# The imaginary half of an autocorrelation product, moved from VectorE to GpSimd by way of a ScalarE copy

## The chip, the cores and the metric

The kernel runs on one core of a Trainium2 chip. The metric is the device time of one launch in microseconds (us). The kernel of before took 1334.72 us, the median of 3 runs (1332.58 to 1335.19).

## What is computed

The program is a decoder of two blocks over 8 batches of 128 positions by 512 channels. The change lies in one step of its first block, the autocorrelation attention of `x` over a context:

```python
qf = jnp.fft.fft(q, axis=2)
kf = jnp.fft.fft(k, axis=2)
corr = jnp.fft.ifft(qf * jnp.conj(kf), axis=2).real
w, idx = jax.lax.top_k(corr.transpose(0, 1, 3, 2), topk)   # topk = int(2 ln 128) = 9
w = jax.nn.softmax(w, axis=-1)
for i in range(topk):
    g = jnp.minimum(idx[:, :, None, :, i] + pos, L - 1)
    out = out + w[:, :, None, :, i] * jnp.take_along_axis(v, g, axis=2)
```

The kernel does this sum with Fourier matrices. The weights (nine entries a channel, zero elsewhere) and the values are both taken to the frequency domain, multiplied there as complex numbers, and taken back by four matmuls.

## The kernel before, in words

The program is written engine by engine: each engine has its own list of instructions, which it works through strictly in order, and semaphores carry the data dependencies. What comes earlier in the program (a state-space model) ends at about 505 us of the span. Then comes the correlation stage, up to about 640 us, with one iteration for each batch b from 0 to 7. Its pieces, with their lines, are these.

On TensorE (PE): `values(b)` (L706, L707) takes the context to its spectrum in banks 1 and 2; `spectra(b)` (L688) does so for x in bank 0; `correlate(b)` (L696, L697) makes the correlation in bank 3; `turn_weights(b)` (L713) transposes the chosen weights; `weights(b)` (L723, L724) takes them to their real spectrum in bank 5 and their imaginary spectrum in bank 6, and raises `wf_done`; `aggregate(b)` (L731) makes four 128x512 matmuls over `m4` into bank 7 and raises `xat_done`. Pieces of the output projection of the stage before (`out_proj`, L647), the small matmuls of the feed-forward layer (`lora_update`, L758), its transposes (`turn`, L739) and its matmuls (`ffn`, L747) stand between them. In iteration b the order is `turn_weights(b)`, `weights(b)`, `correlate(b+1)`, some `out_proj`, `values(b+2)`, `aggregate(b)`, `spectra(b+2)`. In the last iteration `ffn(0)` stands ahead of `turn_weights(7)`, and `ffn(1)` and a `turn` stand ahead of `aggregate(7)`.

On VectorE (DVE): `spectra(b)` (L1830) multiplies the two spectra and waits for PE's `spectra(b)`; `products(b)` (L1873, L1874) multiplies the value spectrum `vri[b % 2]` (128 x 2 x 512, in SBUF) by the real and by the imaginary spectrum of the weights, each read from PSUM, into the four planes of `m4`; `topk(b)` (L1838 to L1863) finds nine maxima and normalises; `out_ln(b)` and `x_ln(b)` add a projection to the token tile and take its statistics (`ln_a`, L1652 to L1656), `ln_b` (L1660) normalises once GpSimd has raised `ln_rs`; `tables(0..2)` are chains of small operations on 4 columns (`tables(2)` is L1630 to L1639). In iteration b the order is `spectra(b+1)`, some `ln_b` and `out_ln`, `x_ln(b-1)`, `products(b)`, `topk(b+1)`. Iteration 4 has `out_ln(7)` behind its `topk(5)`; iteration 6 has `effective()` (L1887) between `products(6)` and `topk(7)`. After the loop stand `ln_b(1,6)`, then `ln_a(2,0)` and `ln_a(2,1)`, the sums behind `ffn(0)` and `ffn(1)`, and only then `x_ln(7)`.

On ScalarE (ACT), all through the helper `av` (L1035): the exponentials of `topk` (`exponents`), six copies in `values(b)`, two of them into `vri[b % 2]`, and the copy of the transposed weights (`turned_weights`).

On GpSimd (POOL) the stage has small work: `rstd` (L1391), one `pow` on one column for each normalisation, in a fixed order; four dequantising rounds k = 0 to 3 (L1483 to L1485), each followed by `rstd(1, k)`; then `rstd(0, 7)` and `table_start` (L1493 to L1496); then for b = 4 to 7 `rstd(1, b)` and two (for b = 7 one) of the doubling rounds of a table (L1504 to L1509). For b = 7 two `bias` additions (L1520) and `rstd(2, 0)` and `rstd(2, 1)` come ahead of `rstd(1, 7)`. `rstd(s, b)` waits for the statistics of DVE's `ln_a(s, b)`. The SP queue issues the loads; none of its waits is on the products.

The loop on GpSimd, as it stands in the kernel of before:

```python
rstd(pool, 0, B - 1)          # waits for DVE's out_ln(7)
table_start()
for b in range(KD, B):        # b = 4..7
    if b == B - 1:
        ...
        for i in range(2): bias(i, i, "fbias")
        for i in range(2): rstd(pool, 2, i)
    rstd(pool, 1, b)
    for k in rounds[2 * (b - KD):2 * (b - KD) + 2]: table_round(k)
```

Of the kernel before, what the change touches and what calls it, by code (L numbers as in the profile page):

```python
# [11 lines left out]
ALU = mybir.AluOpType  # L12
ACT = mybir.ActivationFunctionType
AX = mybir.AxisListType

P = 128
B = 8
L = 128
D = 512
# [126 lines left out]
def decoder_kernel(nc, xT, xtok, ctxT, ctxtok, par, rows, four, win, wx, wdt, wout, qw, sc, ze,  # L146
# [3 lines left out]
    with ExitStack() as ctx:  # L150
# [29 lines left out]
        def part(at, size, parts=P):  # L180
            return arena[0:parts, int(at * KB):int(at * KB) + size]
# [19 lines left out]
        bank = [psum[:, i * 512:(i + 1) * 512] for i in range(8)]  # L201
# [56 lines left out]
        wn = part(36, 2 * D).rearrange("p (s n) -> p s n", s=2)  # L258
        wT = part(40, D)
        vri = [part(at, 2 * D).rearrange("p (i n) -> p i n", i=2) for at in (42, 58)]  # L260
        m4 = part(46, 4 * D).rearrange("p (i n) -> p i n", i=4)
        mx8 = part(54, 4 * 8)
        nx8 = part(54.25, 4 * 8)
# [24 lines left out]
        with nc.sbuf_tensor("dwout_sb", [P, D], F32) as dwout_rows:  # L288
# [47 lines left out]
            "dt_done", "dtu_done", "dA_done", "bu_done", "scan_done", "h_turned", "h_act", "h_dve", "skip_used", "ysum", "y_done",  # L336
            "wout_done",
            "x_sum", "ln_ve", "ln_rs", "x_done",
            "kk_sb", "qf_done", "m12_done", "corr", "rep_done", "ee_done", "wn_done",
            "vf_done", "vri_sb", "wT_done", "wT_sb", "wf_done", "m4_done", "xat_done",  # L340
            "lora_done", "weff_done", "xTt", "xT_sb", "xbias", "ffn_done",
            "tab_a", "tab_b", "tab_c", "tab_d", "tab_e", "tab_done",
# [6 lines left out]
        S = type("S", (), ls)  # L349
# [8 lines left out]
        def lnc(stage, b):  # L358

            if stage < 3:  # L360
                return norms.index((stage, b)) + 1
            if stage == 4 and b >= HB:
                return stage * B + HB + b + 1
            if stage == 5 and b < HB:
                return stage * B - HB + b + 1
            return stage * B + b + 1
# [175 lines left out]
        def _(pe):  # L542
# [122 lines left out]
            for k in range(NR):  # L665
# [6 lines left out]
                if k >= OUT_AT and (k - OUT_AT) % 10 < MD:  # L672
                    b, at = (k - OUT_AT) // 10, (k - OUT_AT) % 10
# [41 lines left out]

            def weights(b):
                if b >= 1:
                    pe.wait_ge(S.m4_done, b)
                else:
                    pe.wait_ge(S.x_sum, lnc(0, HB - 1))  # L720
                    pe.wait_ge(S.y_done, 2 * MD)
                pe.wait_ge(S.wT_sb, b + 1)
                mm(bank[5][:, :], fm["w_re"], wT, start=True, stop=True)  # L723
                mm(bank[6][:, :], fm["w_im"], wT, start=True, stop=True).then_inc(S.wf_done, 1)  # L724

            def aggregate(b):
                pe.wait_ge(S.m4_done, b + 1)
                if b >= 1:
                    pe.wait_ge(S.x_sum, lnc(1, b - 1))
                for i, k in enumerate(("o_rr", "o_ri", "o_ir", "o_ii")):  # L730
                    last = mm(bank[7][:, :], fm[k], m4[:, i, :], start=(i == 0), stop=(i == 3))  # L731
                last.then_inc(S.xat_done, 1)
# [36 lines left out]
            for b in range(B):  # L769
# [10 lines left out]
                if b == 4:  # L780
                    out_proj(7, (4,), 4)
                weights(b)
                if b + 1 < B:
                    correlate(b + 1)
# [189 lines left out]
            for s in range(SLOTS):  # L974
                v, b = s // HB, s % HB
# [57 lines left out]
        def _(act):  # L1033
            def av(o, i, f, **k):
                return nc.scalar.activation(o, i, f, **k)  # L1035
# [166 lines left out]
            def exponents(b):  # L1202
                act.wait_ge(S.rep_done, b + 1)
                for t in range(KD):
                    last = av(ee[:, t * P:(t + 1) * P], bank[3][:, t * P:(t + 1) * P], ACT.Exp, bias=negmax[:, t:t + 1])
                last.then_inc(S.ee_done, 1)

            def values(b):
                act.wait_ge(S.vf_done, b + 1)
                if b >= 1:  # L1210
                    act.wait_ge(S.m12_done, b)
                h = P // 2
                av(kk[0:h, 0, :], bank[1][0:h, :], ACT.Identity)
                av(kk[h:P, 1, :], bank[1][0:h, :], ACT.Identity)
                av(kk[h:P, 0, :], bank[2][0:h, :], ACT.Identity)
                av(kk[0:h, 1, :], bank[2][0:h, :], ACT.Identity).then_inc(S.kk_sb, 1)
                if b >= 2:
                    act.wait_ge(S.m4_done, b - 1)
                av(vri[b % 2][:, 0, :], bank[1][:, :], ACT.Identity)
                av(vri[b % 2][:, 1, :], bank[2][:, :], ACT.Identity).then_inc(S.vri_sb, 1)  # L1220

            def turned_weights(b):
                act.wait_ge(S.wT_done, b + 1)
                av(wT, bank[3][:, :], ACT.Identity).then_inc(S.wT_sb, 1)
# [5 lines left out]
            def turned(b, n, bk):  # L1230
                act.wait_ge(S.xTt, n + 1)
                av(x2T[:, :, b * L:(b + 1) * L], bank[bk][:, :].rearrange("p (k t) -> p k t", k=KD),
                   ACT.Identity).then_inc(S.xT_sb, 1)

            for b in range(B):
                if b == B - 1:
                    turned(0, 0, 0)
                    turned(1, 1, 1)
                turned_weights(b)
                if b + 1 < B:  # L1240
                    exponents(b + 1)
                if b + 2 < B:
                    values(b + 2)
                if b == 0:
                    act.wait_ge(S.tab_a, 1)
                    av(tsm[:, 8, :], tsm[:, 7, :], ACT.Tanh).then_inc(S.tab_b, 1)
# [107 lines left out]
            for s in range(SLOTS):  # L1354
                v, b = s // HB, s % HB
# [32 lines left out]
        def rstd(pool, stage, b):  # L1388

            pool.wait_ge(S.ln_ve, lnc(stage, b))  # L1390
            nc.gpsimd.tensor_tensor(lnrs[:, b:b + 1], lnve[:, b:b + 1], halfneg[:, 0:1], ALU.pow).then_inc(S.ln_rs, 1)  # L1391

        @block.gpsimd
        def _(pool):
            gp = nc.gpsimd
            chain = [0]

            def link(ins):
                chain[0] += 1
                ins.then_inc(S.pool_chain, 1)  # L1400
                pool.wait_ge(S.pool_chain, chain[0])
# [29 lines left out]
            for p in range(MD):  # L1431
                rest_in(p)
                if p >= 4:
                    k = p - 4
# [19 lines left out]
            for i in range(2 * MD * GS):  # L1454
                j, q, e = i // (2 * GS), i // 2 % GS, i % 2
                k = j * NS + q * NG
# [18 lines left out]
            gp.tensor_tensor(tsm[:, 5, :], tsm[:, 4, :], halfneg[:, 0:DEPTH], ALU.pow).then_inc(S.tab_d, 1)  # L1475
            rstd(pool, 0, HB)

            pool.wait_ge(S.sz_in, 64)
            for k in range(KD):
                if k in (0, 2):  # L1480
                    rstd(pool, 0, 5 + k // 2)
                pool.wait_ge(S.qw_in, 16 * (k + 1))
                link(gp.tensor_copy(weff[:, k, :], qw_sb[:, 0, :]))  # L1483
                link(gp.tensor_tensor(weff[:, k, :], weff[:, k, :], sz[:, 1, k, :], ALU.subtract))
                gp.tensor_tensor(weff[:, k, :], weff[:, k, :], sz[:, 0, k, :], ALU.mult).then_inc(S.deq_done, 1)  # L1485
                rstd(pool, 1, k)
# [11 lines left out]
            def table_round(k):  # L1498
                sh = [P, DEPTH, k]
                cl, sl = ctab[:, :, 1:k + 1], stab[:, :, 1:k + 1]  # L1500
                ck, sk = ctab[:, :, k:k + 1].to_broadcast(sh), stab[:, :, k:k + 1].to_broadcast(sh)
                cn, sn = ctab[:, :, k + 1:2 * k + 1], stab[:, :, k + 1:2 * k + 1]
                t0, t1 = ttmp[:, 0, :, 0:k], ttmp[:, 1, :, 0:k]
                gp.tensor_tensor(cn, cl, ck, ALU.mult)  # L1504
                gp.tensor_tensor(t0, sl, sk, ALU.mult)
                gp.tensor_tensor(sn, sl, ck, ALU.mult)
                link(gp.tensor_tensor(t1, cl, sk, ALU.mult))
                gp.tensor_tensor(cn, cn, t0, ALU.subtract)
                link(gp.tensor_tensor(sn, sn, t1, ALU.add))  # L1509
# [7 lines left out]
            def bias(b, n, name):  # L1517

                pool.wait_ge(S.xTt, n + 1)
                gp.tensor_tensor(x_tok[:, b, :], x_tok[:, b, :], rw(name), ALU.add).then_inc(S.xbias, 1)  # L1520
# [4 lines left out]
            for b in range(KD, B):  # L1525
                if b == B - 1:
                    pool.wait_ge(S.row_in, 16)
                    for i in range(2):
                        bias(i, i, "fbias")
                    for i in range(2):  # L1530
                        rstd(pool, 2, i)
                rstd(pool, 1, b)
                for k in rounds[2 * (b - KD):2 * (b - KD) + 2]:
                    table_round(k)
# [35 lines left out]
            for s in range(SLOTS):  # L1570
# [9 lines left out]
                rv, b = (s - 4) // HB, (s - 4) % HB  # L1580
# [7 lines left out]
        def _(dve):  # L1588
            v = nc.vector
# [277 lines left out]
            def products(b):  # L1867
                dve.wait_ge(S.wf_done, b + 1)
                dve.wait_ge(S.vri_sb, b + 1)
                if b >= 1:  # L1870
                    dve.wait_ge(S.xat_done, b)

                v.tensor_tensor(m4[:, 0:2, :], vri[b % 2], bank[5][:, :].unsqueeze(1).to_broadcast([P, 2, D]), ALU.mult)  # L1873
                v.tensor_tensor(m4[:, 2:4, :], vri[b % 2], bank[6][:, :].unsqueeze(1).to_broadcast([P, 2, D]),  # L1874
                                ALU.mult).then_inc(S.m4_done, 1)

            def out_ln(b):
# [208 lines left out]
            for s in range(SLOTS):  # L2086
# [10 lines left out]
                if 4 <= s < NU * HB + 4:  # L2097
                    r = s - 4
                    rv, rb = r // HB, r % HB
                    if rv % NKV == NKV - 1:  # L2100
                        b = (rv // NKV) * HB + rb
# [79 lines left out]
```

## Time and profile before

| | before |
|---|---|
| median of 3 runs | 1334.72 us |
| profiled execution, its own time | 1333.96 us |
| its span, first to last instruction | 1332.2 us |
| PE busy | 1236.0 us (93%) |
| DVE busy | 968.5 us (73%) |
| ACT busy | 748.2 us (56%) |
| POOL busy | 674.8 us (51%) |
| mean granted TensorE clock | 0.986 of full |

Times in views are microseconds from the start of the span. Busy shares are averages over stages; what the stage of the change is limited by has to be read from its own rows. The chain of waits is the sequence of work that ended last, followed back from the end; an instruction that stands in it would move the end if it moved, until something else comes later. Matmuls are pipelined, so in the timeline a matmul's record begins up to 0.2 us ahead of the same piece in the chain.

### The profile page before, as it was taken

What the parts mean: (1) busy time and instruction counts of PE and PEld (TensorE: products, weight loads), DVE (VectorE), ACT (ScalarE), POOL (GpSimd) and SP (SyncE); (2) the same over time, 40 slices, a digit from 0 to 9 for tenths busy, and PEclk for the clock granted to TensorE, in tenths of its full rate; (3) what the DMA queues carried; (4) which work ended last, traced back from release to release, by engine and by line L of the source; (5) the groups of instructions that cost most, each with busy time, mean ns of one, the idle gap of its engine ahead of it and who ended that gap; (6) DMA issues with size and microseconds to landing.
All of it is one profiled execution on the core that took longest, in us unless ns stands there. A gap on an engine that the chain in (4) does not pass through costs nothing.

```text
span 1332.2 us, 18653 instructions
## 1 busy us (share of the span) xinstructions
PE 1236.0 (93%) x6464; PEld 925.4 (69%) x6464; DVE 968.5 (73%) x1770; ACT 748.2 (56%) x1478; POOL 674.8 (51%) x535
## 2 busy tenths in 40 slices
PE   6997899999998988998998999999998999999995
PEld 5876677767777764444565547888887888888874
DVE  4785798999999997898657766655554675666676
ACT  5479898989998983332133235544544445444441
POOL 4128988888988870222842126443433543333331
PEclk9999899999999999999999999999998999999999
DMA  6003200122220015002300103222221221111110
GB/s 182 12 26 139 75 25 25 35 93 88 88 72 1 1 56 136 16 9 85 144 9 16 40 24 103 80 73 71 68 75 48 80 79 65 63 64 64 48 48 32
DMA packets 37213, 81.92 MB, mean 61 GB/s; under 512 B 3808, under 2 KB 8160, under 8 KB 35200
## 3 DMA queue, kind: packets, MB, share of 16 engines
q1 hardware_dynamic: 37120, 80.72, 18.5%
q8 instruction: 53, 0.87, 0.3%
q14 instruction: 40, 0.33, 0.1%
HBM read 74.35 MB, written 6.36 MB: 61 GB/s over the span
## 4 chain that ended last, share of the span: by engine, by line
PE 68%; DVE 19%; ACT 6%; issue 5%; POOL 1%; DMA 1%; SPq 1%; DVEq 0%; POOLq 0%; ACTq 0%
PE psum L547 10%; PE psum L549 10%; PE psum L548 10%; PE psum L622 7%; PE psum L636 6%; PE psum L982 4%; DVE arena L1747 4%; PE psum L660 3%; PE psum L647 3%; ACT arena L1035 3%; PE psum L747 2%; PE psum L1001 2%; PE psum L731 1%; DVE lnst L1654 1%; PE psum L871 1%
## 5 line engine op out<-in xcount | busy, mean ns | idle before, releaser
L1471 POOL TENSOR_TENSOR arena<-arena 128x1024 f32<-128x1024 f32 x128 | 300.4, 2370 | 42.7 <-DVE arena L1747 42.5
L1407 POOL TENSOR_TENSOR w_split<-arena,w_split 128x512 fp32r<-128x512 f32 x128 | 168.1, 1333 | 280.3 <-ACT w_split L1035 280.3
L1747 DVE TENSOR_TENSOR_SCAN arena<-psum,arena 128x512 f32<-128x512 f32 x256 | 292.3, 1204 | 15.2 <-ACT psum L1035 15.2
L622 PEld LDWEIGHTS psum<-prm,arena 128*128 128x128 f32 x1024 | 118.7, 142 | 110.3 <-issue 61.8
L1035 ACT ACTIVATE psum<-arena,amat 128x508 f32<-128x508 f32 x256 | 173.3, 709 | 30.4 <-DVE arena L1747 29.4
L622 PE MATMUL psum<-prm,arena 128*128 128x128 f32 x1024 | 148.9, 280 | 38.4 <-DVE arena L1747 34.7
L1035 ACT ACTIVATE arena<-psum,ssmC 128x256 f32<-128x256 f32 x448 | 177.5, 484 | 10.8 <-PE psum L622 10.7
L1035 ACT ACTIVATE arena<-arena 128x512 f32<-128x512 f32 (+2 forms) x86 | 62.8, 734 | 210.1 <-DVE arena L2043 209.1
L1035 ACT ACTIVATE arena<-psum,prm 128x512 f32<-128x512 f32 (+1 forms) x130 | 91.1, 708 | 148.6 <-PE psum L549 70.0
L636 PE MATMUL psum<-prm,arena 128*128 128x128 f32 x1024 | 134.1, 273 | 0.1
L636 PEld LDWEIGHTS psum<-prm,arena 128*128 128x128 f32 x1024 | 117.0, 141 | 0.4 <-ACT arena L1035 0.3
L547 PE MATMUL psum<-x_split,w_split 128*128 128x512 f32 x256 | 106.3, 415 | 2.9 <-DVE x_split L2029 2.8
L1035 ACT ACTIVATE arena<-psum 128x512 f32<-128x512 f32 (+4 forms) x108 | 57.8, 563 | 82.7 <-PE psum L739 33.3
L1391 POOL TENSOR_TENSOR lnrs<-lnve,halfneg 128x1 f32<-128x1 f32 x48 | 28.4, 591 | 143.3 <-DVE lnve L1656 143.3
L549 PE MATMUL psum<-x_split,w_split 128*128 128x512 f32 x256 | 100.9, 394 | 0.0
L548 PE MATMUL psum<-x_split,w_split 128*128 128x512 f32 x256 | 100.8, 394 | 0.0
L547 PE MATMUL psum<-w_split,o_split 128*128 128x512 f32 x256 | 100.7, 394 | 0.0
L549 PE MATMUL psum<-w_split,o_split 128*128 128x512 f32 x256 | 100.1, 391 | 0.0
L548 PE MATMUL psum<-w_split,o_split 128*128 128x512 f32 x256 | 99.6, 389 | 0.0
L2040 DVE TENSOR_REDUCE amax<-psum 128x4 f32<-128x512 f32 x64 | 44.1, 688 | 52.4 <-PE psum L982 52.4
L2059 DVE TENSOR_TENSOR ssmT<-psum,p_split 128x512 fp32r<-128x512 f32 x64 | 44.2, 691 | 51.5 <-ACT p_split L1035 51.4
L2049 DVE TENSOR_REDUCE asum<-arena 128x4 f32<-128x512 f32 x64 | 43.9, 686 | 44.0 <-ACT arena L1035 44.0
(230 smaller groups left out, 2544.0 us busy)
## 6 DMA issues: line engine op xcount, KB each, us to landing
arena<-wq SPq DMA_DIRECT2D x64, 256.0 KB, 2.6
arena<-wo SPq DMA_DIRECT2D x64, 256.0 KB, 2.8
arena<-bc_scratch SPq DMA_DIRECT2D x8, 1024.0 KB, 5.2
arena<-win SPq DMA_DIRECT2D x16, 256.0 KB, 2.7
v_keep<-row SPq DMA_DIRECT2D x16, 256.0 KB, 2.1
arena<-v_keep SPq DMA_DIRECT2D x1, 4096.0 KB, 12.8
arena<-xT SPq DMA_DIRECT2D x8, 256.0 KB, 5.5
x_tok<-wv SPq DMA_DIRECT2D x1, 2048.0 KB, 7.7
```

The lines of the kernel that those rows point to most:

```text
L547: mm(o, l[0], r[0], start=start, stop=False)
L548: mm(o, l[0], r[1], start=False, stop=False)
L549: return mm(o, l[1], r[0], start=False, stop=stop)
L622: last = nc.tensor.transpose(hT[:, c, b % 2, e, :], hst[:, (2 * k + e) % 4, b * L:(b + 1) * L], ident)
L636: last = mm(bank[6 + e][:, b * L:(b + 1) * L], hTs[:, k % 2, b, e, :], ident, start=(n == 0 and b == 0), stop=(n == NS - 1 and b == HB - 1 ...
L982: last = mm(bank[1][:, j * P:(j + 1) * P], qT[:, v % 2, j, b * L:(b + 1) * L], KT[:, v % NKV, gb * L:(gb + 1) * L], start=True, stop=True)
L1035: return nc.scalar.activation(o, i, f, **k)
L1407: gp.tensor_tensor(out_, whole, hi.bitcast(F32), ALU.subtract).then_inc(done, 1)
L1471: gp.tensor_tensor(bu[:, i % 4, :, :], dtu[:, (2 * j + e) % 4, :].unsqueeze(1).to_broadcast([P, NG, HT]), Brep[:, q * NG:(q + 1) * NG, :], ...
L1747: v.tensor_tensor_scan(hst[:, i % 4, :], decay_bank(i), bu[:, (k // NG * 2 + e) % 4, k % NG, :], 0.0, ALU.mult, ALU.add).then_inc(S.scan_d ...
L2040: link(v.tensor_reduce(amax[:, :], ps, AX.X, ALU.max))
L2059: v.tensor_tensor(p_lo[:, r % 2, :], bank[2][:, :], p_hi[:, r % 2, :].bitcast(F32), ALU.subtract).then_inc(S.p_rest, 1)
```

## The change

`wim` is a new tile of 128x512 in SBUF. ScalarE copies bank 6, the weights' imaginary spectrum, into it, behind `turned_weights(b)` in its list. GpSimd multiplies `vri[b % 2]` by `wim` into planes 2 and 3 of `m4` (`imaginary(b)`). VectorE keeps planes 0 and 1. Both engines raise `m4_done`, which so counts two for each batch, and every wait on it is doubled.

```diff
+        wim = part(62, D)
...
             def weights(b):
                 if b >= 1:
-                    pe.wait_ge(S.m4_done, b)
+                    pe.wait_ge(S.m4_done, 2 * b)
...
             def aggregate(b):
-                pe.wait_ge(S.m4_done, b + 1)
+                pe.wait_ge(S.m4_done, 2 * (b + 1))
...
                 if b >= 2:
-                    act.wait_ge(S.m4_done, b - 1)
+                    act.wait_ge(S.m4_done, 2 * (b - 1))
                 av(vri[b % 2][:, 0, :], bank[1][:, :], ACT.Identity)
...
                 turned_weights(b)
+                act.wait_ge(S.wf_done, b + 1)
+                if b >= 1:
+                    act.wait_ge(S.m4_done, 2 * b)
+                av(wim, bank[6][:, :], ACT.Identity).then_inc(S.wim_sb, 1)
                 if b + 1 < B:
                     exponents(b + 1)
...
+            def imaginary(b):
+
+                pool.wait_ge(S.wim_sb, b + 1)
+                pool.wait_ge(S.vri_sb, b + 1)
+                if b >= 1:
+                    pool.wait_ge(S.xat_done, b)
+                gp.tensor_tensor(m4[:, 2:4, :], vri[b % 2], wim.unsqueeze(1).to_broadcast([P, 2, D]),
+                                 ALU.mult).then_inc(S.m4_done, 1)
+
             pool.wait_ge(S.sz_in, 64)
             for k in range(KD):
+                imaginary(k)
                 if k in (0, 2):
                     rstd(pool, 0, 5 + k // 2)
                 pool.wait_ge(S.qw_in, 16 * (k + 1))
...
                     for i in range(2):
                         rstd(pool, 2, i)
+                imaginary(b)
                 rstd(pool, 1, b)
                 for k in rounds[2 * (b - KD):2 * (b - KD) + 2]:
                     table_round(k)
...
-                v.tensor_tensor(m4[:, 0:2, :], vri[b % 2], bank[5][:, :].unsqueeze(1).to_broadcast([P, 2, D]), ALU.mult)
-                v.tensor_tensor(m4[:, 2:4, :], vri[b % 2], bank[6][:, :].unsqueeze(1).to_broadcast([P, 2, D]),
+                v.tensor_tensor(m4[:, 0:2, :], vri[b % 2], bank[5][:, :].unsqueeze(1).to_broadcast([P, 2, D]),
                                 ALU.mult).then_inc(S.m4_done, 1)
```

## Rows read from the trace of the kernel before

**Rows 1.** The page's part 4: shares of the chain that ended last, by engine
```profile
PE 68%; DVE 19%; ACT 6%; issue 5%; POOL 1%; DMA 1%; SPq 1%; DVEq 0%; POOLq 0%; ACTq 0%
```

**Rows 2.** Busy time in stretches: us, then PE, PEld, DVE, ACT, POOL, clock, DMA
```profile
560.00:590.00 30.00, 28.39 (x96) 14.61 (x95) 28.43 (x84) 9.66 (x22) 8.32 (x9) 1.00 0.04 10
```

**Rows 3.** Lines L1874 and L1471 by themselves: ns min/median/max, first and last start
```profile
L1874 DVE TENSOR_TENSOR arena<-arena,psum x8: 1214/1214/1216, 528.1 to 634.8; 128x1024 f32<-128x1024 f32 x8
L1471 POOL TENSOR_TENSOR arena<-arena x128: 2340/2365/2585, 122.3 to 490.9; 128x1024 f32<-128x1024 f32 x128
```

**Rows 4.** Chain of waits, 550 to 640 us: start us, us, what
```profile
550.25 3.43 PE psum L731 x8
...
553.69 0.87 PE psum L688 x2
...
569.20 0.64 PE psum L713 x4
...
587.70 1.22 DVE arena L1873
...
598.47 1.22 DVE arena L1830
...
601.84 1.22 DVE arena L1873
...
611.53 0.64 PE psum L713 x4
...
612.93 1.97 PE psum L723 x2
614.90 1.68 PE psum L724 x2
...
637.49 3.44 PE psum L731 x8
```

**Rows 5.** Timeline of GpSimd, 525 to 642 us: start us, us, engine, line, operation, tiles
```profile
525.05 0.55 POOL L1391 TENSOR_TENSOR lnrs<-lnve,halfneg 128x1 f32<-128x1 f32 x1
...
547.56 0.55 POOL L1391 TENSOR_TENSOR lnrs<-lnve,halfneg 128x1 f32<-128x1 f32 x1
...
558.58 0.55 POOL L1391 TENSOR_TENSOR lnrs<-lnve,halfneg 128x1 f32<-128x1 f32 x1 [4.65 <-DVE lnve L1656]
...
598.60 0.55 POOL L1391 TENSOR_TENSOR lnrs<-lnve,halfneg 128x1 f32<-128x1 f32 x1 [10.22 <-DVE lnve L1656]
...
599.29 0.19 POOL L1496 COPY arena<-tsm 128x4 f32<-128x4 f32 x1
602.03 0.55 POOL L1391 TENSOR_TENSOR lnrs<-lnve,halfneg 128x1 f32<-128x1 f32 x1 [2.54 <-DVE lnve L1656]
...
604.95 0.21 POOL L1509 TENSOR_TENSOR arena<-arena 128x8 f32<-128x8 f32 x1
...
631.79 0.55 POOL L1391 TENSOR_TENSOR lnrs<-lnve,halfneg 128x1 f32<-128x1 f32 x1 [13.73 <-DVE lnve L1656]
...
641.86 0.55 POOL L1391 TENSOR_TENSOR lnrs<-lnve,halfneg 128x1 f32<-128x1 f32 x1 [1.20 <-DVE lnve L1656]
```

**Rows 6.** Timeline of VectorE in tables(2) and products(2), 558 to 561 us
```profile
558.42 0.15 DVE L1630 TENSOR_TENSOR tsm<-tsm 128x4 f32<-128x4 f32 x1
...
559.97 1.22 DVE L1873 TENSOR_TENSOR arena<-arena,psum 128x1024 f32<-128x1024 f32 x1
```

**Rows 7.** Timeline at 1275 us: a VectorE operation with two SBUF inputs beside GpSimd
```profile
1275.14 1.28 POOL L1407 TENSOR_TENSOR w_split<-arena,w_split 128x512 fp32r<-128x512 f32 x1 [4.44 <-ACT w_split L1035]
...
1275.51 1.47 DVE L2053 TENSOR_TENSOR arena<-arena,ainv 128x512 f32<-128x512 f32 x1
```

**Rows 8.** Timeline of TensorE, weights(5) and turn_weights(6)
```profile
598.54 1.10 PE L723 MATMUL psum<-arena 128*128 128x512 f32 x2 [0.78 <-ACT arena L1035]
...
611.53 0.63 PE L713 MATMUL psum<-prm,arena 128*128 128x128 f32 x4 [2.73 <-DVE arena L1863]
```

**Rows 9.** Busy time at 613 us: us, PE, PEld, DVE, ACT, POOL, clock, DMA
```profile
613.00:614.00 1.00, 1.00 (x2) 0.48 (x3) 0.96 (x2) 0.00 (x0) 0.00 (x0) 0.51 0.00 0
```

More of the change, by code:

```diff
@@ L338, in decoder_kernel @@
             "x_sum", "ln_ve", "ln_rs", "x_done",
-            "kk_sb", "qf_done", "m12_done", "corr", "rep_done", "ee_done", "wn_done",
+            "kk_sb", "wim_sb", "qf_done", "m12_done", "corr", "rep_done", "ee_done", "wn_done",
             "vf_done", "vri_sb", "wT_done", "wT_sb", "wf_done", "m4_done", "xat_done",
```

## The prediction

> **What bounds the kernel now.** I read the page's chain first: PE holds 68% of it and DVE 19%, GpSimd 1% [rows 1]. That average hides the stage of the change, so I went to the busy time of a stretch inside it: from 560 to 590 us PE is busy 28.39 us of 30 and DVE 28.43, GpSimd only 8.32 [rows 2]. Two engines are the bound there together. The chain of waits says the same: it changes between them, and DVE's product and PE's matmuls take turns in it, from 587.70 on for one [rows 4]. So a shorter DVE list can gain something, and the idle share of GpSimd looks like free room. But GpSimd works its list in order, so the question is where each `imaginary(b)` stands in it and what stands ahead of it. That is read from GpSimd's timeline [rows 5], against the start of the `aggregate` that waits for it [rows 4].
>
> **What is removed.** L1874, 8 times. One takes 1.21 us [rows 3]; the next operation starts 1.13 us behind its start, since records overlap, so 1.13 is what goes. If DVE were the bound throughout, that would be 8 x 1.13 = 9.0 us.
>
> **What is added.** GpSimd gets 8 products of 128x1024 f32 with one operand broadcast. L1471 is the same form: 2.37 us, at most 2.59 [rows 3]. ScalarE gets 8 copies of one bank. They are hidden: the equal copy of `turned_weights`, with the steps to and from it, fits into the 0.78 us that PE idles between L713 and L723 [rows 8], and GpSimd takes up each product later than that behind wf_done in every iteration below (b = 0, where it does not, has the time). A new wait of ScalarE on wf_done has behind it only `exponents(b+1)`, which DVE's maxima release several us later. No DMA is added and SP waits for none of this.
>
> **The walk, batch by batch.** I shift the starts of before by what has been gained or lost so far. GpSimd to PE is taken as 0.15 us, the step that the chain shows from other engines to PE.
>
> b = 0: GpSimd is free at 525.6 [rows 5], the product ends at 528.0, and PE wants it behind out_proj, 7 us later. Nothing. DVE's gain goes into its wait for PE's next `spectra`.
>
> b = 1: GpSimd comes to it after rstd(1,0) at 547.56. It ends at 547.56 + 0.5 + 2.37 = 550.43, PE starts at 550.6, where before it started at 550.25 [rows 4, 5]. PE, which starts `spectra(3)` behind it (553.69), is 0.35 us late, and DVE with it.
>
> b = 2: rstd(1,1) starts at 558.58 + 0.35, so the product runs from 559.4 to 561.8. DVE is then in `tables(2)`, shifted by 0.35 from 558.42 and up to products(2) at 559.97 [rows 6], small operations most of which read two SBUF tiles. What such an operation does beside a running GpSimd one stands at 1275 us [rows 7]: L2053 took 1.47 us and ended 0.56 us behind it, where the shortest of its kind takes 0.69; it did its work only when GpSimd had finished. Against that stands that the short `pow` at 525.05 held nobody visibly. I take the first [rows 7], since 2.37 us of streaming is nearer to that than a pow on one column. The rest of the table chain then starts at 561.8, `products(2)` at 562.6 in place of 559.97, 2.65 late, and less the 1.13 saved `topk(3)` is 1.5 late. Its end releases PE's `turn_weights(3)` (569.20) [rows 4]. **+1.5 us.** Bounds: without the block PE bounds instead, 0.6 early; with a second block it is 2 us more.
>
> The Trainium skill, "SBUF — State Buffer", section "SBUF: two separate sides", states that VectorE and GpSimd share one pair of ports as an exclusive lock, for a VectorE operation with two SBUF inputs against a GpSimd one that reads SBUF, whatever its size. By this rule the term is +1.5, and by the pow row read alone -0.6; the trace at 1275 us agrees with the rule.
>
> b = 3: the product runs behind rstd(1,2), and ends 0.2 to 0.4 us ahead of PE. Nothing; the shift stays.
>
> b = 4 is the large one. `imaginary(4)` stands behind `rstd(0, 7)`, which waits for `out_ln(7)`, which DVE does only after `topk(5)`. products(4) starts at 587.70 and that rstd at 598.60 [rows 4, 5]: 10.9 us, now 10.9 - 1.13 = 9.77. Then rstd and table_start 0.88 (to 599.48), the product 2.37, the step 0.15, `aggregate(4)` 3.43, `spectra(6)` 0.87, the step to DVE 0.05: 17.52 us from products(4) to DVE's spectra(6). Before it was 598.47 - 587.70 = 10.77. **+6.75 us.** PE idles some 8 us, and while it does `vri`'s next copies wait too, without effect.
>
> b = 5: products(5) to `turn_weights(6)` was 611.53 - 601.84 = 9.69 us, bound by DVE's topk. Now rstd(1,4) starts 0.19 behind products(5), and two table rounds, to 605.16, stand ahead of the product: 0.19 + 3.13 + 2.37 + 0.15, then aggregate 3.43 and spectra(7) 0.87 make 10.14. **+0.45 us.**
>
> b = 6: before, PE's clock fell after 2.73 us of idle [rows 8] and 0.78 more, with a short transpose between: the granted clock at 613 us is 0.51, which is the 1.2 GHz level [rows 9]; L723's and L724's pairs took 1.97 + 1.68 = 3.65 us [rows 4], where at the level of 2.4 GHz they take 1.10 [rows 8] and 0.87, as L688's [rows 4], together 1.97. Now PE has 4.3 us of work just ahead of it, so I take the loss as gone: **-1.7 us** (bounds -1.7 and 0). The product ends just with lora_update, no more.
>
> b = 7: `imaginary(7)` stands behind rstd(1,6), two rounds, two bias additions and rstd(2,0), rstd(2,1). From 631.79 to 641.86 that is 10.07 us [rows 5], then 0.5 + 2.37 + 0.15 = 13.1 us to `aggregate(7)`. Before, that started at 637.49, 5.7 us behind 631.79. **+7.4 us.** From there PE is continuous to the end of the stage, so it stays.
>
> Sum: 1.5 + 6.75 + 0.45 - 1.7 + 7.4 = 14.4 us. **Clock:** the two new holes, some 8 us ahead of aggregate(4) and 7 us ahead of aggregate(7), are longer than what made the clock fall at 613 us; I charge each 1.7 us, what that fall cost (bounds 0 and twice that), +3.4. Total +17.8. The profiled execution took 1333.96 us, 0.8 under the median of its runs; the forecast is 1333.96 + 17.8 = 1351.8 us.
>
> **Rivals.**
>
> A. The order on GpSimd holds, but there is no block and little clock loss: 14.4 - 2.1 + 0 to 1.7, 1346 to 1348 us. For: small operations ran beside the pow. Against: [rows 7].
>
> B. More is lost: low clock for twice as long at each hole (+3.4), a further fall at the hole of b = 5 (some 2.4 us, +1.7), GpSimd's products blocked by DVE's two-input steps of topk. 1353.5 to 1357 us.
>
> C. GpSimd runs beside DVE and only DVE's list counts. DVE's 9.0 us come off where DVE bounds, which the chain shows for b = 2 to 5 [rows 4], about half: 1329 us; with all of it 1325. It needs each product to be done 2.5 us or so behind wf_done. It turns on the position of rstd(0,7): it would hold if `out_ln(7)` were ahead of topk(5). The list says it is not.
>
> D. The change costs and gains nothing: PE alone bounds, and the products are done in time. 1333 to 1336. The 7 us at b = 4 and b = 7 speak against it equally.
>
> **Chances.** The main case 0.55, A 0.2, B 0.17, C 0.05, D 0.03. About 0.2% (2.7 us) is what a measurement of this kernel can tell. The range takes in A and B: 1346 to 1357. Faster 0.05, same 0.03, slower 0.92.
>
> **What would show it.** In the changed kernel's timeline, GpSimd's new product should start right behind L1496's table copies for b = 4 and behind rstd(2,1) for b = 7; PE should name GpSimd's new line as the releaser of L731, with waits near 8 and 7 us; the granted clock should be near 0.5 at both; one operation of tables(2) should last some 2 us. ACT's exponents should move with DVE alone. Wrong it would be if PE's wait for those two aggregates were under 2 us each, if the chain did not pass through GpSimd, or if the stages behind 664 us had changed their length.

## The result

The changed kernel took 1359.99 us (median; 1357.98 to 1360.71 in 4 runs), the kernel before 1334.4 us beside it: a ratio of 1.0182, with a 95% interval of 1.0163 to 1.0201. The forecast was 1351.8 us, in a range of 1346 to 1357. The direction and the mechanism came as forecast, the size did not: the time lies 3 us above the range. The profiled execution took 1357.98 us, 24.0 more than the profiled execution of before (17.8 were forecast).

The page of the changed kernel shows its span, granted clock and chain. The lines of code have moved: `aggregate` is now L732, VectorE's `spectra` L1846, the ScalarE helper L1036, GpSimd's `rstd` L1396; the new product is L1489.

```profile
span 1356.2 us, 18675 instructions
...
PEclk9998999999999999988999999999998999999999
...
PE 65%; DVE 19%; ACT 5%; issue 5%; POOL 3%; DMA 1%; SPq 1%; DVEq 0%; POOLq 0%; ACTq 0%
```

GpSimd has gone from 1% of the chain [rows 1] to 3%, and the clock string has two 8s side by side at 576 to 644 us, where the kernel before has 9s. Who waits for the new product is told by its own line and by TensorE's waits from 545 to 662 us (us in total, times, longest):

```profile
L1489 POOL TENSOR_TENSOR arena<-arena x8: 2340/2344/2351, 525.8 to 655.7; 128x1024 f32<-128x1024 f32 x8
```

```profile
PE psum L732 <- POOL arena L1489: 15.7, 5, 7.7
PE psum L714 <- DVE arena L1879: 2.7, 2, 2.1
```

The product itself takes 2.34 us, as its form in [rows 3] promised. TensorE waits 15.7 us for it, in five waits. It is not that the product is slow; it starts late. GpSimd's timeline shows what stands ahead of it for batch 4 and for batch 7:

```profile
591.41 0.55 POOL L1396 TENSOR_TENSOR lnrs<-lnve,halfneg 128x1 f32<-128x1 f32 x1 [7.44 <-DVE lnve L1672]
601.52 0.55 POOL L1396 TENSOR_TENSOR lnrs<-lnve,halfneg 128x1 f32<-128x1 f32 x1 [9.55 <-DVE lnve L1672]
...
602.49 2.34 POOL L1489 TENSOR_TENSOR arena<-arena 128x1024 f32<-128x1024 f32 x1
...
644.05 0.55 POOL L1396 TENSOR_TENSOR lnrs<-lnve,halfneg 128x1 f32<-128x1 f32 x1 [9.35 <-DVE lnve L1672]
...
655.19 0.55 POOL L1396 TENSOR_TENSOR lnrs<-lnve,halfneg 128x1 f32<-128x1 f32 x1 [1.20 <-DVE lnve L1672]
655.70 2.34 POOL L1489 TENSOR_TENSOR arena<-arena 128x1024 f32<-128x1024 f32 x1
```

By 601.52 GpSimd had idled 9.55 us in its queue, with the data of product 4 ready since ScalarE's copy of 591.10 to 591.70 us: what it waited for is the statistics of `out_ln(7)`. These rows answer to 598.60 and to 631.79 and 641.86 in [rows 5].

**A measure for one stage.** The rest of the kernel (the span less the stage) took 1177.1 to 1183.1 us in the profiled executions of the runs below, though none edits it, so I measure the stage alone: from the start of the first `spectra` on VectorE to the start of the last feed-forward matmul. Both are read from the lines by themselves ("first and last start"), here of the changed kernel:

```profile
L1846 DVE TENSOR_TENSOR arena<-arena,psum x8: 1214/1222/1223, 509.7 to 625.6; 128x1024 f32<-128x1024 f32 x8
```

```profile
L748 PE MATMUL psum<-arena x64: 592/592/697, 642.4 to 685.0; 128*128 128x512 f32 x64
```

685.0 - 509.7 = 175.3 us. In the kernel before it is 662.7 - 509.5 = 153.2. So 22.1 of the 24.0 us are in this stage. Each stage length comes from one profiled execution: a fall of the clock that some executions have and others have not would stand in it with 1.7 us or more. One of the ten runs of e3_four took 3217.93 us for a cause that is not known; it does not enter the ratio. The shifts against before, counted from the first `spectra`, at the points of the forecast:

| up to | forecast, its part | measured, its part | measured, in all |
|---|---|---|---|
| turn_weights(3) | +1.5 | +1.4 | +1.4 |
| VectorE's spectra(5) | 0 | +2.0 | +3.4 |
| VectorE's spectra(6) | +6.75 and 1.7 of clock | +9.9 | +13.3 |
| turn_weights(6) | +0.45 | +0.3 | +13.6 |
| end of the stage | -1.7, +7.4 and 1.7 of clock | +8.5 | +22.1 |
| rest of the kernel | 0 | +1.9 | +24.0 |

### The profile page after: what moved, and what is told of

Its sections match the earlier page's. It is cut to its first block, busy times and chain, and to the rows that moved or that the text cites. A ratio compares the mean times of both kernels' runs of the same rounds, so it can differ in the third digit from the quotient of the medians.

```text
span 1356.2 us, 18675 instructions
## 1 busy us (share of the span) xinstructions
PE 1245.8 (92%) x6464; PEld 928.9 (68%) x6464; DVE 969.7 (72%) x1762; ACT 753.8 (56%) x1486; POOL 693.1 (51%) x543
## 4 chain that ended last, share of the span: by engine, by line
PE 65%; DVE 19%; ACT 5%; issue 5%; POOL 3%; DMA 1%; SPq 1%; DVEq 0%; POOLq 0%; ACTq 0%
PE psum L548 10%; PE psum L550 10%; PE psum L549 10%; PE psum L623 6%; PE psum L637 6%; DVE arena L1763 4%; PE psum L983 4%; PE psum L661 3%; ACT arena L1036 3%; PE psum L648 3%; PE psum L732 2%; PE psum L748 2%; PE psum L1002 2%; DVE lnst L1670 1%; PE psum L872 1%
## 5 line engine op out<-in xcount | busy, mean ns | idle before, releaser
L1036 ACT ACTIVATE psum<-arena,amat 128x508 f32<-128x508 f32 x256 | 173.1, 708 | 29.9 <-DVE arena L1763 28.9
L1036 ACT ACTIVATE arena<-psum,ssmC 128x256 f32<-128x256 f32 x448 | 177.7, 483 | 11.6 <-PE psum L623 11.6
L1036 ACT ACTIVATE arena<-arena 128x512 f32<-128x512 f32 (+2 forms) x86 | 62.9, 734 | 210.1 <-DVE arena L2058 209.1
L1036 ACT ACTIVATE arena<-psum,prm 128x512 f32<-128x512 f32 (+1 forms) x130 | 91.3, 709 | 150.3 <-PE psum L550 71.8
L637 PE MATMUL psum<-prm,arena 128*128 128x128 f32 x1024 | 134.3, 274 | 0.1
L1036 ACT ACTIVATE arena<-psum 128x512 f32<-128x512 f32 (+4 forms) x116 | 62.7, 565 | 122.3 <-PE psum L740 40.7
L1396 POOL TENSOR_TENSOR lnrs<-lnve,halfneg 128x1 f32<-128x1 f32 x48 | 28.4, 592 | 151.6 <-DVE lnve L1672 151.6
```

The lines of the kernel that those rows point to most:

```text
L637: last = mm(bank[6 + e][:, b * L:(b + 1) * L], hTs[:, k % 2, b, e, :], ident, start=(n == 0 and b == 0), stop=(n == NS - 1 and b == HB - 1 ...
```

## The experiments

Each ran beside the kernel before on the same chip. The stage length is from the profile of the run.

| run | stage us | median us (runs) | ratio to before |
|---|---|---|---|
| before | 153.2 | | |
| the change | 175.3 | 1359.99 (4) | 1.0182 |
| e1_order | 159.4 | 1343.82 (10) | 1.0036 |
| e3_four | 165.0 | 1347.7 (10) | 1.0055 |
| e4_seven | 168.8 | 1353.67 (4) | 1.0101 |
| e2_early | 158.2 | 1338.3 (10) | 0.9998 |
| e9_warm | 170.9 | 1352.55 (4) | 1.0119 |
| e14_warm | 169.9 | 1350.52 (8) | 1.0097 |
| e6_tables | 153.3 | 1336.19 (10) | 1.0001 |
| e7_control | 152.8 | 1340.89 (8) | 1.0034 |
| e5_negmax | 156.0 | 1338.58 (10) | 1.0008 |
| e11_both | 159.6 | 1342.03 (10) | 1.0040 |
| e13_tail | 158.2 | 1337.69 (10) | 0.9988 |
| e8_five | 155.1 | 1338.28 (10) | 1.0009 |
| e12_plain | 152.9 | 1334.98 (12) | 0.9996 |
| e10_clear | 151.8 | 1334.65 (12) | 0.9978 |

The kernel before spread from 1332 to 1348 us on these chips, so the intervals of the ratios are 0.2 to 0.5% wide to each side, and differences of a microsecond or two are read from the stage.

### The order of GpSimd's list

e1_order, only the place of the calls on GpSimd:

```diff
+            imaginary(KD)
             rstd(pool, 0, B - 1)
             table_start()
...
                     for i in range(2):
                         rstd(pool, 2, i)
-                imaginary(b)
                 rstd(pool, 1, b)
+                if b + 1 < B:
+                    imaginary(b + 1)
                 for k in rounds[2 * (b - KD):2 * (b - KD) + 2]:
```

> GpSimd's list alone is reordered: the product of batch 4 stands ahead of rstd(0,7), those of 5 to 7 ahead of the table rounds (7 also ahead of the bias additions). Theory Q (what stands ahead of the product in GpSimd's list costs the time): the holes ahead of aggregate(4), (5) and (7) and their low clock go, and what is left is the port block and the clock fall of batches 2 and 3, some 3.4 us: 1336 to 1340 us. Theory G (a product on GpSimd is itself too slow, 2.4 us and a copy against 1.1): every batch still pays, 1346 us or more. Theory P (port blocks are most of it): 1348 us or more.

Stage 159.4 us, so 15.9 of the 22.1 us are gone with nothing but four calls, `imaginary(4)` to `imaginary(7)`, in other places. TensorE's wait for the product fell to 0.2 us. The absolute time, 1343.82 us (ratio 1.0036, 1.0009 to 1.0062), lies between theory Q and theory G. From turn_weights(7) to the end of the stage it took 35.1 us for 32.4 before, a further 2.7 us where I had not looked. TensorE's waits from 600 to 680 us:

```profile
PE psum L714 <- DVE arena L1881: 2.5, 1, 2.5
PE psum L748 <- DVE x_tok L1670: 2.5, 1, 2.5
```

The second line is new: feed-forward matmuls wait for a normalisation behind GpSimd's bias addition, which the products now push back (e13_tail below).

e3_four moves only the product of batch 4 (`imaginary(KD)` ahead of `rstd(pool, 0, B - 1)`, and `if b > KD` on the call in the loop):

> Only the product of batch 4 is moved, ahead of rstd(0,7). Theory Q: the hole of about 8 us there and the low clock behind it (aggregate(4) took 6.11 us in place of 3.43) go, 8 to 10 us off, 1349 to 1352 us. Theory G: no more than 3 us off.

10.3 us less in the stage; the median, 1347.70 us, is 1.3 us under the forecast. e4_seven moves only that of batch 7:

```diff
+                if b == B - 1:
+                    imaginary(b)
                 if b == B - 1:
                     pool.wait_ge(S.row_in, 16)
...
-                imaginary(b)
+                if b < B - 1:
+                    imaginary(b)
```

> Only the product of batch 7 is moved, ahead of the two bias additions and rstd(2,0), rstd(2,1), still behind the table rounds of batch 6. Theory Q: the bias additions and the two rstd are 6.5 us of the hole; with the low clock behind it 5 to 8 us off, 1351 to 1355 us. Theory G: no more than 2 us off.

6.5 us less, with the median of 1353.67 us in the forecast. The two holes are thus shown one at a time, each with the low clock behind it. The profiled executions took 1344.4 and 1348.9 us; in them the rest of the kernel was 3.3 and 2.6 us shorter than in the changed kernel.

### The clock behind the holes

Busy time in the changed kernel's stretches of low clock (us, PE, PEld, DVE, ACT, POOL, granted clock, DMA):

```profile
572.00:575.40 3.40, 3.16 (x4) 1.51 (x5) 3.23 (x8) 0.10 (x1) 1.23 (x3) 0.53 0.00 0
575.40:599.00 23.60, 21.15 (x75) 10.83 (x73) 21.81 (x70) 8.96 (x21) 8.88 (x8) 1.00 0.05 11
599.30:609.50 10.20, 4.62 (x6) 2.04 (x7) 2.04 (x5) 1.24 (x3) 3.23 (x6) 0.51 0.01 2
609.60:633.00 23.40, 19.46 (x73) 10.50 (x73) 17.92 (x47) 6.62 (x14) 8.74 (x28) 1.00 0.00 1
633.50:640.30 6.80, 6.37 (x9) 2.45 (x8) 6.16 (x30) 1.14 (x4) 1.20 (x1) 0.51 0.63 217
657.40:660.80 3.40, 2.70 (x3) 1.18 (x4) 0.00 (x0) 0.00 (x0) 0.64 (x1) 0.52 0.00 0
```

Four falls to the level of 1.2 GHz, where the kernel before has one in this stage [rows 9]. What they do to `aggregate`, which takes 3.43 us in the chain at 2.4 GHz [rows 4] and 3.70 as the timeline shows a group that had to start anew:

```profile
604.88 6.11 PE L732 MATMUL psum<-arena 128*128 128x512 f32 x8 [7.74 <-POOL arena L1489]
...
634.75 6.53 PE L732 MATMUL psum<-arena 128*128 128x512 f32 x8 [0.43 <-POOL arena L1489]
...
658.10 5.11 PE L732 MATMUL psum<-arena 128*128 128x512 f32 x8 [4.94 <-POOL arena L1489]
```

e9_warm fills the holes with matmuls that `aggregate` overwrites:

```diff
             def aggregate(b):
-                pe.wait_ge(S.m4_done, 2 * (b + 1))
                 if b >= 1:
                     pe.wait_ge(S.x_sum, lnc(1, b - 1))
+                if b in (4, 7):
+                    for i in range({4: 8, 7: 5}[b]):
+                        mm(bank[7][:, :], fm["o_rr"], ctx_sb[:, b, :], start=True, stop=True)
+                pe.wait_ge(S.m4_done, 2 * (b + 1))
```

> The changed kernel with work put into TensorE's two largest holes: 8 extra matmuls of 128x512 ahead of aggregate(4) and 5 ahead of aggregate(7), into the bank that the aggregate overwrites, so they add nothing to the result and end before GpSimd's product does. Theory C (low clock behind the holes is 4 to 6 us of the loss): aggregate(4) takes 3.4 to 3.7 us in place of 6.11, aggregate(7) the same in place of 5.11, the stage from the first spectra to the last feed-forward matmul 175.3 - 4 to 6 = 169 to 171 us. Rival (the fill only takes the place of idle time and the clock does not matter): 175 us or more.

Stage 170.9 us, 4.4 less, with 13 more matmuls in it, as theory C had it:

```profile
606.76 3.70 PE L735 MATMUL psum<-arena 128*128 128x512 f32 x8 [0.87 <-POOL arena L1492]
...
634.36 6.25 PE L735 MATMUL psum<-arena 128*128 128x512 f32 x8
...
656.89 3.70 PE L735 MATMUL psum<-arena 128*128 128x512 f32 x8
```

The filled ones run at full speed, the unfilled aggregate(6) stays slow. So idle TensorE time costs twice here, once as a wait and once as slow matmuls behind it. e14_warm fills two more (`{4: 8, 5: 2, 6: 2, 7: 5}`):

> e9_warm (stage 170.9 us) with two more extra matmuls ahead of aggregate(5), where TensorE still idled 2.5 us, and two ahead of aggregate(6). If the low clock over aggregate(6), which took 5.9 us there, came from the hole ahead of aggregate(5), it goes and the stage is 167 to 169 us. If it comes from the 16-row matmuls of lora_update, which run just ahead of it, it stays and the stage is 170.5 to 173.

aggregate(6) was fast, but the stage was 169.9 us, between the two forecasts. turn_weights(7) came 1.8 us earlier than in e9_warm, and 0.9 of that was lost again behind products(7), where VectorE's `ln_b` was held beside GpSimd's bias additions and in e9_warm hardly was. First e9_warm, then e14_warm:

```profile
649.78 0.60 DVE L1679 TENSOR_SCALAR x_tok<-x_tok,lnmv,lnrs 128x512 f32<-128x512 f32 x1
```

```profile
644.14 1.53 DVE L1679 TENSOR_SCALAR x_tok<-x_tok,lnmv,lnrs 128x512 f32<-128x512 f32 x1
```

Since both the fill of batch 5 and that ahead of aggregate(6) were new, the run does not tell which of them kept the clock up.

### The shared port

e2_early leaves batches 4 to 7 to VectorE:

```diff
+                if b in (0, 1, 2, 3):
+                    act.wait_ge(S.wf_done, b + 1)
...
             def imaginary(b):
+                if b not in (0, 1, 2, 3):
+                    return
...
+                if b not in (0, 1, 2, 3):
+                    v.tensor_tensor(m4[:, 2:4, :], vri[b % 2], bank[6][:, :].unsqueeze(1).to_broadcast([P, 2, D]),
+                                    ALU.mult).then_inc(S.m4_done, 1)
```

> GpSimd makes the product for batches 0 to 3 only, in the order of the change; VectorE makes both for 4 to 7. Theory Q with port blocks: the tables chain of batch 2, the maxima of batch 4 and one fall of the clock cost 3 to 5 us, less what VectorE saves later: 1336 to 1339 us. If blocks of small operations cost nothing: 1332 to 1335 us.

1338.3 us is in the forecast of theory Q, but the ratio, 0.9998 (0.9970 to 1.0026), tells nothing; the stage does: 158.2 us, 5.0 longer. In it GpSimd's products are never late (TensorE waits 0.2 us for them). What is late is VectorE, as in the changed kernel in `tables(2)`:

```profile
559.66 0.15 DVE L1651 TENSOR_TENSOR tsm<-tsm,prm 64x4 f32<-64x4 f32 x1
559.85 2.27 DVE L1652 TENSOR_TENSOR tsm<-tsm 64x4 f32<-64x4 f32 x1
562.15 0.16 DVE L1653 TENSOR_TENSOR tsm<-tsm,prm 64x4 f32<-64x4 f32 x1
```

An operation on four columns, 0.15 us in its like, lasted 2.27 us, to the end of GpSimd's product (559.75 to 562.1). TensorE then idles for turn_weights(3) and its clock falls. In e2_early:

```profile
570.55 0.63 PE L714 MATMUL psum<-prm,arena 128*128 128x128 f32 x4 [2.10 <-DVE arena L1882]
571.96 2.04 PE L724 MATMUL psum<-arena 128*128 128x512 f32 x2 [0.78 <-ACT arena L1036]
```

e6_tables takes the chain out from beside the product, and e7_control does the same in the kernel before:

```diff
             for b in range(B):
+                if b == 1:
+                    plc = tables(2)
...
                     x_ln(1)
-                    plc = tables(2)
```

> GpSimd makes the products of batches 0 to 3 as in e2_early (stage 158.2 us), with the tables chain of batch 2 moved to the start of batch 1, so that it no longer runs beside GpSimd's product. Port-block theory: the 2.3 us step of that chain is gone, the stage is 1.5 to 3.5 us shorter, 154.7 to 156.7. Rival (the delay of batch 2 is from late data): 157.5 to 159.

> The tables chain of batch 2 moved to the start of batch 1 in the kernel before, nothing on GpSimd: whether this move gains by itself. If e6_tables gained from the port block alone, the stage here is 152.7 to 153.6 us; if the move gains by itself, 149 to 151.

153.3 us, 4.9 less than e2_early and more than the 1.5 to 3.5 I had put. 3.2 of it are there by spectra(5): the block went, and with it the clock fall at 572 us. The other 1.6 came between turn_weights(6) and turn_weights(7), where e2_early has a clock fall over aggregate(6) (5.40 us) and e6_tables has none (3.70); that this too hangs on the block is not shown. The control is at 152.8 us: the move by itself gives 0.5, and four products on GpSimd still gain nothing beside it. The control's median, 1340.89 us (ratio 1.0034), does not fit this: its eight runs took 1334.81 to 1343.10 us and the profiled one 1334.92, and what made the others longer stays open.

In the changed kernel two more small operations, of one SBUF input each, are held at batch 3:

```profile
578.63 2.12 DVE L1856 TENSOR_SCALAR arena<-arena 128x4 f32<-128x4 f32 x1
...
582.75 1.25 DVE L1867 COPY arena<-arena 128x4 f32<-128x4 f32 x1
```

In the kernel before these two take 0.17 and 0.18 us. The first ended with GpSimd's product of batch 3 (578.38 to 580.72 us). What the second ended with is not the product but a step of the dequantising round behind it, which the product has pushed to this place:

```profile
582.71 1.26 POOL L1500 TENSOR_TENSOR arena<-arena 128x512 f32<-128x512 f32 x1
```

e5_negmax lets ScalarE make the first:

```diff
-                v.tensor_scalar(negmax.unsqueeze(2), mx8.rearrange("p (t n) -> p t n", t=KD)[:, :, 0:1], -1.0, None,
-                                ALU.mult)
...
                 act.wait_ge(S.rep_done, b + 1)
+                link(av(negmax.unsqueeze(2), mx8.rearrange("p (t n) -> p t n", t=KD)[:, :, 0:1], ACT.Identity, scale=-1.0))
```

> e2_early with the negated maxima, a VectorE operation on four columns that took 2.12 us beside GpSimd's product of batch 3 in the changed kernel, made by ScalarE. Port-block theory: 1 to 2.2 us shorter than 158.2, 156 to 157.2. Rival: 158 or more, as the block moves to the next VectorE operation.

156.0 us, in the forecast, but for the most part by another cause: up to spectra(5) it is 0.4 us ahead of e2_early (77.4 against 77.8 us after the first spectra). Of the other 1.8 us, 1.7 are one clock fall fewer, the one over aggregate(6) (3.70 us for 5.40). So the block of batch 3 was real and mostly covered by TensorE, which was late itself.

### Both together, and the end of the stage

e11_both is e1_order with the move of e6_tables.

> All eight products on GpSimd, the order of e1_order and the tables chain moved as in e6_tables. If queue order, port blocks and the clock falls behind them are all of the loss, the stage is 159.4 less 4 to 5 = 154.5 to 155.5 us, and what is left is GpSimd's bias additions coming late at the end of the stage (2 to 3 us in e1_order). If GpSimd's slower product costs by itself in each batch: 157 us or more.

A miss: 159.6 us, by its number in the rival's range. But up to turn_weights(6), with six products done, it is at 102.4 us after the first spectra where before has 102.1: not each batch pays. From there on it lost 6.0 us. 1.6 of them lie ahead of turn_weights(7), with a clock fall over aggregate(6) (5.40 us); 4.5 lie behind it, at this wait and a clock fall behind it:

```profile
657.04 3.65 PE L748 MATMUL psum<-arena 128*128 128x512 f32 x4 [2.50 <-DVE x_tok L1670]
```

e13_tail gives the product of batch 7 back to VectorE (the sets of e2_early, with 0 to 6):

> e11_both (stage 159.6 us) with the product of batch 7 given back to VectorE, so that GpSimd's list has nothing new ahead of the two bias additions. If the end of the stage is long in e11_both because GpSimd's product of batch 7 pushes back its table rounds and bias additions (a 2.5 us wait in the feed-forward matmuls and the clock fall behind it), both go: stage 154.5 to 156. If it is long for another reason: 158 or more.

From turn_weights(7) to the end it took 32.4 us, as before, where e11_both had 36.9: that cause is shown. The stage, 158.2 us, is outside the forecast and in the rival's range all the same, since the clock fell for 6.8 us twice in this execution (at 612 and 622 us; aggregate(6) took 6.40 us), which the kernel before has for 3.4 us once.

### Where a product on GpSimd can pay

e8_five moves batch 5 alone, the one behind which TensorE waited 2.73 us for VectorE [rows 8].

> GpSimd makes the product of batch 5 alone, ahead of its table rounds. That batch is where VectorE's topk made TensorE wait 2.7 us in the kernel before. Theory Q: 1.1 us off that wait, perhaps the clock fall at 613 us too: stage 150.4 to 152.3 us in place of 153.2. Theory G: 153.2 or more.

Theory Q failed at 155.1 us: turn_weights(6) came no earlier (102.6 us for 102.1). The timelines of GpSimd and VectorE say why:

```profile
602.45 2.35 POOL L1492 TENSOR_TENSOR arena<-arena 128x1024 f32<-128x1024 f32 x1
```

```profile
602.88 2.20 DVE L1681 TENSOR_SCALAR x_tok<-x_tok,lnmv,lnrs 128x512 f32<-128x512 f32 x1
```

`ln_b(0, 7)`, 0.54 us by itself, stood right behind VectorE's half and ended only behind the product. What VectorE had saved, 1.1 us, it paid back there with 0.5 more; the other 1.4 us of the stage go with a clock fall over aggregate(6) (5.40 us). e10_clear is e8_five with the edit of e5_negmax and

```diff
                 if b == 5:
+                    ln_b(0, 7)
                     ln_b(1, 3)
                     x_ln(4)
...
-                if b == 5:
-                    ln_b(0, 7)
```

and e12_plain has these two edits in the kernel before.

> GpSimd makes the product of batch 5 alone, ahead of its table rounds, as in e8_five (stage 155.1 us), and what ran blocked beside it is out of its way: ln_b(0,7), which took 2.20 us in e8_five, stands ahead of x_ln(4), and the negated maxima are made by ScalarE. Port-block theory: turn_weights(6) comes 1.1 to 1.3 us earlier than in the kernel before (102.0 us after the first spectra), the stage is 150.3 to 152.2 us where before has 153.2. Theory G: no earlier than before, stage 153 or more.

> The same two moves (ln_b(0,7) and the negated maxima) in the kernel before, nothing on GpSimd: what of e10_clear is due to them. 0.15 us a batch where VectorE bounds: stage 152.6 to 153.3 us.

turn_weights(6) came 100.6 us after the first spectra, 1.4 earlier than before and 1.2 earlier than in the control (101.8), and the stage took 151.8 us against 152.9 in the control, both in their forecasts. The times: 1334.65 us (12 runs) to 1335.78, ratio 0.9978 (0.9957 to 1.0000). The control's median is 1334.98 us. By their times the two kernels can't be told apart; the gain is read from one execution's stage each.

## Why the prediction was right, and where it was wrong

**The walk by batches held, but for b = 3.** The block in `tables(2)` was forecast from [rows 7] as +1.5 us and measured as +1.4. From the rstd of batch 4 to aggregate(4) I had 3.40 us and the trace has 604.88 - 601.52 = 3.36. Batch 5 came at +0.3 for +0.45. Batch 6, up to rstd(1,6): 134.3 - 122.3 = 12.0 us of shift, less the 13.6 at turn_weights(6), is -1.6 for -1.7. e1_order, e3_four and e4_seven show that the order of the list is the cause of most of it. On the signs: the waits of 7.7 and 4.9 us, the clock at 0.51 and 0.52 and the 2.27 us step in `tables(2)` came. The hole ahead of aggregate(7) was 4.9 us and not 7, as the slow aggregate(6) (6.53 us) had made TensorE itself late.

Of the Trainium skill's rule, "SBUF — State Buffer", section "SBUF: two separate sides": the 2.27 us of L1652 and the 2.20 us of L1681 agree with it, the second for an operation that takes 0.54 us by itself and has one SBUF tile as its input, a kind that the same section counts in when it runs in a two-port mode. In which mode it ran no row here shows.

**The step that failed is the clock term**, "I charge each 1.7 us", and with it, for b = 3, "Nothing; the shift stays". The kind of cost was right and its size was not. I counted two holes at 1.7 us each, 3.4 us. Measured on the path are three: 1.7 us at weights(3), which I had at nothing (2.04 + 1.59 us in the chain where 1.10 + 0.87 are due), 2.7 at aggregate(4) (6.11 for 3.43) and 1.7 at aggregate(7) (5.11 for 3.43). That is 6.0 for 3.4. A block on VectorE that I had priced alone brought the first: it left TensorE idle for 2.1 us, and I did not ask what that idle time would do. e6_tables takes the block out, and this fall is gone.

Three smaller terms were at nothing in the sum. From rstd(1,6) to aggregate(7) the trace has 14.05 us for my 13.1. On this path stand the slow aggregate(6) (6.53 us for 3.43), which made products(7) late, and VectorE's `ln_b` behind it, held beside GpSimd's bias additions; their shares are not separated:

```profile
650.46 1.17 DVE L1676 TENSOR_SCALAR x_tok<-x_tok,lnmv,lnrs 128x512 f32<-128x512 f32 x1
```

The operations held in topk(4) add 0.3. In front of topk(5) VectorE, earlier by the product it no longer makes, waits 0.4 us for TensorE's correlation, so the saving of 1.13 us is not all kept. With the 2.6 us of the clock these make 4.3 of the 6.2 us by which the profiled execution missed. The last 1.9 us are in the rest of the kernel, less than that rest differs between runs (1177.1 to 1183.1 us). My own sign for a wrong prediction, a changed length behind 664 us, was met by this much. The changed kernel has one more fall there, at 818 us (1.7 us); that it follows from the change is not shown, since e2_early and e8_five have one there too.

The median of the changed kernel is 2.0 us above its profiled execution. Those 2 us have no profile and stay open.

**The rivals.** A fell, as the block and the clock loss are both there. B was nearest and had too little room, and its terms came only in part: the clock stayed low longer at the hole of b = 4 (10.2 us in all) but not at b = 7; at the hole of b = 5 it did not fall (1.00 from 609.6 to 633 us); GpSimd's products were not held up (2340 to 2351 ns). C and D fell. That the offload can gain where it is not in the way rests on e10_clear: 1.1 us of stage for one batch out of eight, in one execution.

## What to carry to other kernels

Before an operation is moved to an engine that looks idle, read its list in order, find what stands ahead of the new place and what *that* waits for: here 15.9 of 22.1 us came from four products standing behind other waits. Then look at what runs on VectorE during a long GpSimd operation: even four columns can cost as long as the GpSimd operation has left. And price each stretch in which TensorE is left idle once more for the slower matmuls behind it.

## What the runs showed that was not expected

The granted clock also fell with TensorE busy. In e10_clear the columns (us, PE, PEld, DVE, ACT, POOL, granted clock, DMA) read:

```profile
613.00:616.00 3.00, 3.00 (x20) 2.27 (x19) 2.71 (x5) 0.00 (x0) 2.02 (x9) 1.00 0.00 0
616.00:619.50 3.50, 3.50 (x9) 1.41 (x8) 2.52 (x5) 0.00 (x0) 0.96 (x5) 1.00 0.00 0
619.70:623.10 3.40, 3.40 (x6) 1.45 (x5) 3.30 (x18) 1.04 (x5) 0.00 (x0) 0.55 0.66 169
```

```profile
615.58 3.70 PE L759 MATMUL psum<-arena 16*128 16x512 f32 x8
619.20 5.40 PE L732 MATMUL psum<-arena 128*128 128x512 f32 x8
```

TensorE had no idle stretch between 613 and 619.5 us, but its matmuls from 615.6 on had 16 rows only (`lora_update`), and the full ones behind them ran at 1.2 GHz. e2_early, e8_five, e11_both and e13_tail have a fall at the same place. The kernel before has the same 16-row matmuls without one behind them, and in e14_warm there was none either. Whether the 16 rows bring it was not tried by itself.
